# Sums of squares as 128 rows of 64 steps, two buffers for norms and masked scores, new orders in the mixer and the feed-forward stage

## The chip, the cores and the metric

The kernel runs on one core of a Trainium2 chip. The metric is the device time of one execution in microseconds (us). The engines are PE (TensorE: matmuls, with its weight loads shown apart as PEld), DVE (VectorE), ACT (ScalarE), POOL (GpSimd) and SP (SyncE, which here only issues transfers). Each takes its instructions in order and waits for others through semaphores; ACT, POOL and SP also issue DMAs.

## The reference

Eight rows of 512 steps by 256 channels pass a state-space mixer and a feed-forward layer, each behind a layernorm and followed by one. Cut to what matters:

```
x = x + layernorm(attn(layernorm(x)))          # x: 8 rows of 512 steps x 256
x = x + layernorm(ffn(layernorm(x)))

attn:  proj = x @ W_in.T                        # gate 512, value 512, 64 step parameters
       value = silu(dw_bias + sum(xp[:, k:k + T] * dw_weight[:, k] for k in range(4)))
       dt = clip(softplus(params[..., 0] + dt_bias), 1e-4, 0.1)
       bc = (value @ W_bc.T).reshape(B, T, 32, 4, 32)
       bc = bc / (sqrt(sum(bc * bc, axis=-1)) + 1e-8)
       per step:  z = S * (z - dt * A * s + dt * (Bz u));  s = s + dt * z + dt * (Bx u)
                  y = Cz . z + Cx . s
       out = ((y + skip * value) * silu(gate)) @ W_out.T
ffn:   out = gelu(x @ ternary(W1).T + b1) @ ternary(W2).T + b2
```

`Bz, Bx, Cz, Cx` are the four parts of `bc`, 32 heads by 32 states each, every one divided by its own norm over the 32 states.

## The kernel before

Three stages run one after the other. `project` makes the value, the gate and the step sizes, row after row, and leaves them in DRAM. The change does not touch it. `mix` is the mixer, `ffn` the output projection, the residual and the feed-forward layer.

In `mix` the 32 heads are 8 groups of 4; a group fills 128 partitions (4 heads by 32 states). A row is worked in two halves of four groups ("first" to "first + 3"), and a pass over a half is called a phase here: 16 phases in all. In a phase the DVE works on the half at hand and prepares the next one (its first group is called "then" in the code).

Products: PE multiplies `w_bc` by `valT` in units, four units (j = 0..3) per group, each four matmuls of 128x512 (L700). ACT takes each unit out of PSUM twice, squared into `sq` and as it is into `raw` (`evacuate`). PE runs 21 units ahead of the phase.

Norms: after the first unit of the next group PE sums the squares (`sum_squares`, L685: four matmuls with `head_sum`, 32 rows by 512 steps each, into 128 partitions of which 16 matter). ACT takes the square root (L825) into `rows`. SP packs the 16 rows of 512 into `compact`, 128 rows of 64, by four DMAs (`compact_norms`). DVE adds the epsilon, inverts, and multiplies by `factor` (`scales`, L1027 to L1034). SP stores `compact` to DRAM, waits for it, and loads it back spread over the partitions into `scale`: four DMAs for the B parts (`input_scales`), and, once DVE has used those, four for the C parts (`output_scales`). DVE multiplies `raw` by it: `scale_inputs` (L1042) and `scale_outputs` (L1050). There is one `compact`, one `scale` and one `factor`.

The rest of a phase: DVE runs 128 small steps of a recurrence (`step_psi`, L1016 and L1020) woven between its other work by a count of nominal costs (`advance`). `keys` makes the B side of a group (L1079, L1083); PE transposes it (L722) and forms the state terms (L738). `det_sums`, `coefficients` and `states` (L1156 to L1165) make the block states of the half, which ACT spreads into `Xb` (L877). `queries` makes the C side (L1093 to L1116). PE then computes the scores of a group (`scores_and_unit`, L759, with one product unit in two pieces between), DVE multiplies them by the causal mask (`mask`, L1124) into the one tile `g`, and PE makes the outputs (`outputs`: L778 from `g`, L784 from `Xb`). Scores of a group wait for the mask of the group before; the mask waits for the outputs of the group before, as there is one `g`.

What sets the order is the program order that is written out in `phase` for DVE and in the bodies of the other engines.

In `ffn` one row after the other is gated (`y * gate + svg`, two operations of 128x2048 on POOL, L1387 and L1389), projected (L1407), normalised and added (`first_residual`), normalised again (`second_norm`), split into a high and a low part, multiplied (L1436), passed through gelu on ACT (L1494), split again, multiplied by the second weight (L1449), given its bias, normalised and added (the end of the DVE body). A loop over pairs of rows runs this, with the first and last two rows written out.

## Time and profile before

| what | us |
|---|---|
| median of 3 runs | 2638.85 |
| lowest, highest | 2637.96, 2643.87 |
| the profiled execution | 2637.77 |
| its span in the trace | 2636.1 |
| of it `ffn` | 2308 to 2636 |
| det inverse (one per phase), first to last | 449.63 to 2239.5 |

The profiled execution lies 1.1 us under the median and 1.7 us over its own span. Busy times are for one engine; an engine that waits is idle in them. A number in square brackets behind a row of a timeline is the idle time before it, with what ended it.

### The profile page before, as it was taken

The numbers are of one execution on the slowest core, as the hardware profiler recorded it, in microseconds if no ns is written. First come the engines' busy times: TensorE is split into PE (matmuls) and PEld (weight loads), VectorE is DVE, ScalarE is ACT, GpSimd is POOL, SyncE is SP. The second block draws the span as 40 slices with busy tenths as digits, with TensorE's granted clock in tenths as the row PEclk, the third lists the DMA queues.
The fourth block names the chain that finished last, engine by engine and source line by source line (L and its number), as shares of the span: only waits on it lengthen the run. The fifth ranks groups of instructions, "written<-read, shape, count | busy, mean of one in ns | idle before, by whom it ended". The sixth has DMA issues, their size and how long they took to land. (4 is left out here: it accounts for less than half of the span.)

```text
span 2636.1 us, 66597 instructions
## 1 busy us (share of the span) xinstructions
PE 2092.6 (79%) x25890; PEld 1258.7 (48%) x25890; DVE 1921.2 (73%) x4396; ACT 956.8 (36%) x1905; POOL 385.6 (15%) x604
## 2 busy tenths in 40 slices
PE   5777485887888988888878789998988887728886
PEld 2333132454454545444544445454544446626675
DVE  5777257786869686878878697968778797456775
ACT  3555222333333333343433333343333332104444
POOL 0000111111111111111111111111111110042210
PEclk9888697988889889988888888898898985568887
DMA  3555542534353535444353535454453533073300
GB/s 96 172 171 163 148 127 82 134 100 131 96 137 99 131 103 136 109 111 131 104 129 97 135 95 130 115 135 111 107 134 101 137 83 85 14 253 127 127 25 24
DMA packets 240466, 306.05 MB, mean 116 GB/s; under 512 B 124960, under 2 KB 141344, under 8 KB 231968
## 3 DMA queue, kind: packets, MB, share of 16 engines
q1 hardware_dynamic: 134496, 152.84, 20.2%
q10 hardware_dynamic: 85056, 94.40, 12.8%
q0 software_dynamic: 20608, 54.56, 8.2%
q8 instruction: 212, 3.47, 0.6%
q14 instruction: 94, 0.77, 0.1%
HBM read 240.85 MB, written 57.68 MB: 113 GB/s over the span
## 5 line engine op out<-in xcount | busy, mean ns | idle before, releaser
L700 PE MATMUL m_ps_a<-m_valT,m_w_bc 128*128 128x512 f32 x2048 | 1037.3, 651 | 59.5 <-DMA m_valT<-scratch_valT 49.2
L700 PEld LDWEIGHTS m_ps_a<-m_valT,m_w_bc 128*128 128x128 f32 x2048 | 397.3, 206 | 472.9 <-issue 443.7
L651 POOL DMA_DIRECT2D m_shear<-scratch_shear x512 | 274.3, 537 | 1564.8 <-DVE m_psi L1020 1452.8
L835 ACT ACTIVATE m_sq<-m_ps_a 128x512 f32<-128x512 f32 x256 | 153.1, 598 | 651.7 <-PE m_ps_a L700 651.7
L759 PE MATMUL m_ps_g<-m_raw 32*64 32x64 f32 x8192 | 185.9, 249 | 166.9 <-DVE m_g L1124 141.3
L1020 DVE TENSOR_TENSOR m_psi<-m_psi,m_prod 128x128 f32<-128x128 f32 x1024 | 294.0, 287 | 19.6
L1016 DVE TENSOR_TENSOR m_prod<-m_psi,m_shear 128x128 f32<-128x128 f32 x1024 | 293.0, 286 | 18.0
L759 PEld LDWEIGHTS m_ps_g<-m_raw 32*64 32x64 f32 x8192 | 165.0, 159 | 268.4 <-issue 265.9
L1042 DVE TENSOR_TENSOR m_raw<-m_raw,m_scale 128x1024 f32<-128x1024 f32 x64 | 78.4, 1224 | 239.0 <-DMA m_scale<-scratch_norm 230.3
L784 PE MATMUL m_ps_k<-m_raw,m_Xb 128*112 128x64 f32 x1024 | 177.1, 306 | 0.0
L1079 DVE TENSOR_TENSOR m_part<-m_raw,m_psi 128x1024 f32<-128x1024 f32 x128 | 155.6, 1218 | 13.7 <-issue 13.2
L224 PE MATMUL ps_w<-p_xnT,w_in 128*128 128x512 f32 x256 | 130.5, 663 | 41.1 <-ACT vraw L282 36.0
L1110 DVE TENSOR_TENSOR m_part<-m_raw,m_psi 128x1024 f32<-128x1024 f32 x128 | 155.6, 1218 | 0.1
L784 PEld LDWEIGHTS m_ps_k<-m_raw,m_Xb 128*112 128x112 f32 x1024 | 150.9, 216 | 8.5 <-issue 3.7
L837 ACT ACTIVATE m_raw<-m_ps_a 128x512 f32<-128x512 f32 x256 | 152.5, 596 | 0.0
L897 ACT ACTIVATE m_y<-m_ps_y 112x256 f32<-112x256 f32 x64 | 24.6, 384 | 305.1 <-PE m_ps_k L784 305.1
L1124 DVE TENSOR_TENSOR m_g<-m_ps_g,m_causal 128x1024 f32<-128x1024 f32 x64 | 78.0, 1219 | 74.4 <-PE m_ps_k L784 74.3
L784 PE MATMUL m_ps_y<-m_raw,m_Xb 128*112 128x64 f32 x768 | 130.4, 303 | 0.0
L877 ACT ACTIVATE m_Xb<-m_X 32x224 f32<-32x224 f32 x256 | 98.7, 386 | 74.9 <-DVE m_X L1165 71.8
L1050 DVE TENSOR_TENSOR m_raw<-m_raw,m_scale 128x1024 f32<-128x1024 f32 x64 | 78.1, 1220 | 60.5 <-DMA m_scale<-scratch_norm 60.5
L784 PEld LDWEIGHTS m_ps_y<-m_raw,m_Xb 128*112 128x112 f32 x768 | 114.1, 218 | 0.0
L224 PEld LDWEIGHTS ps_w<-p_xnT,w_in 128*128 128x128 f32 x256 | 52.2, 212 | 115.8 <-issue 66.0
(147 smaller groups left out, 2847.5 us busy)
## 6 DMA issues: line engine op xcount, KB each, us to landing
m_scale<-scratch_norm SPq DMA_DIRECT2D x512, 128.0 KB
m_w_bc<-in_w_bcT ACTq DMA_DIRECT2D x252, 256.0 KB, 3.5
m_shear<-scratch_shear POOLq DMA_DIRECT2D x512, 64.0 KB, 2.9
m_det<-scratch_ab POOLq DMA_DIRECT2D x64, 256.0 KB, 5.6
scratch_yT<-m_y ACTq DMA_DIRECT2D x64, 224.0 KB, 2.8
...
```

What stands on the lines that cost most here:

```text
L224: mm = pe.matmul(ps_w[i % BANKS].ap(), w_in[:, k, col:col + P], xnT[:, k, :], start=(k == 0), stop=(k == KD - 1))
L651: pool.dma_start(shear[h * N:(h + 1) * N, w % 2].rearrange("p k g t -> p k (g t)"), spread(src)).then_inc(into.sem, into.step)
L700: mm = pe.matmul(ps_a[j % 2].ap(), w_bc[:, j, kt, :], valT[:, kt, :], start=(kt == 0), stop=(kt == KI - 1))
L759: mm = pe.matmul(ps_g[odd * C:(odd + 1) * C, at:at + C], raw[heads, group, p_, cols], raw[heads, group, NJ - 1 - p_, cols], start=(p_ == 0 ...
L784: mm = pe.matmul(ps_y[c % 2][0:ROWS, c // 2 * C:(c // 2 + 1) * C], Xb[:, c - 1, p_, :], raw[:, group, NJ - 1 - p_, c * C:(c + 1) * C], sta ...
L835: act.activation(sq[:, j, :], ps_a[j % 2].ap(), ACT.Square).then_inc(sq_ready.sem, sq_ready.step)
L837: act.activation(raw[:, group % HG, j, :], ps_a[j % 2].ap(), ACT.Copy).then_inc(raw_ready.sem, raw_ready.step)
L877: ins = act.activation(Xb[heads, :, :, h * N:h * N + DH], X[heads, 0:NC - 1, :, group % HALF, :], ACT.Copy)
L1016: dve.tensor_tensor(prod.ap().rearrange("p k g r -> p (k g) r"), psi_kt[of_half][:, :, t, :], window.unsqueeze(2).to_broadcast([P, 2 * HAL ...
L1020: ins = dve.tensor_tensor(psi_t[of_half][:, :, :, t + 1, :], psi_t[of_half][:, :, :, t, :], prod[:, ::-1, :, :], ALU.add)
L1079: dve.tensor_tensor(in_pairs(part[:, k]), pairs(raw[:, slot, k, :]), psi[:, half % 2, k, g_, :, at:at + C, :], ALU.mult).then_inc(own.sem, ...
L1110: dve.tensor_tensor(in_pairs(part[:, k]), pairs(raw[:, group, 3 - k, :]), psi[:, half, k, g_, :, 1:, :], ALU.mult).then_inc(own.sem, own.o ...
```

## The change

In `mix`:
- `sum_squares` uses eight matrices `of_segment`, each of which puts the four heads into other output rows, and 32 matmuls of 64 columns in place of 4 of 512. The result stands in PSUM as 128 rows of 64 steps, the layout of `compact`.
- The square root writes `compact` at once; `compact_norms` and `rows` are gone. `compact` has two buffers, and the square root waits for the store of two groups before.
- The masked scores alternate between `g` and the memory of `kT`, and the mask waits for the outputs of two groups before.
- DVE's order in a phase is new: scalings of the next half come earlier, and the first mask stands inside `states`, after its fourth block.
- SP loads `valT` of the next row tile by tile as the last unit lets each go, behind the scale loads of "then + 2".

In `ffn`: the loop is written out; gating is on DVE and POOL has nothing left; weights are loaded from ACT's queue; the ternary step takes two operations instead of three; the second product comes in two halves with bias and moments after each; the last normalisation of a row moves behind the start of the next.

The diff, cut:

```diff
@@ mix: tiles @@
+        of_segment = sb("of_segment", [P, N // HP, N])
...
-        rows_ = sb("rows", [P, T])
-        compact = sb("compact", [P, SEG])
+        compact = sb("compact", [P, 2, SEG])
...
+        masked = [g.ap(), kT.ap().rearrange("p a (b h c) -> p a b h c", b=2, h=HP)]
@@ mix: SP @@
-                def compact_norms(b, group):
-                    sp.wait_ge(norm_ready.sem, norm_ready.at(b, group))
-                    for j in range(NJ):
-                        sp.dma_start(compact[j * N:(j + 1) * N, :],
-                                     rows_[j * N:j * N + HP, :].rearrange("h (s t) -> h s t", t=SEG)
-                                     ).then_inc(compact_in.sem, compact_in.step)
...
                 def load_valT(b):
                     for kt in range(KI):
+                        if not (isinstance(b, int) and b == 0):
+                            sp.wait_ge(val_used.sem, val_used.at(b - 1, kt)) if kt < KI - 1 else sp.wait_ge(a_made.sem, a_made.at(b - 1, UNITS - 1))
                         sp.dma_start(valT[:, kt, :], dram["valT"][b, :, kt, :]).then_inc(val_in[kt].sem, val_in[kt].step)
...
-                    compact_norms(b, group)
...
                     sp.dma_start(dram["norm"][group % 2].rearrange("r (s t) -> (r s) t", t=SEG),
-                                 compact.ap()).then_inc(rows_stored.sem, rows_stored.step)
+                                 compact[:, group % 2, :]).then_inc(rows_stored.sem, rows_stored.step)
...
                             norm_rows(b, then + 2)
+                            input_scales(b, then + 2)
                         if half == 0 and not last:
-                            sp.wait_ge(a_made.sem, a_made.at(b, UNITS - 1))
                             load_valT(b + 1)
                         if more:
-                            input_scales(b, then + 2)
                             output_scales(b, then + 2)
                             norm_rows(b, then + 3)
-                        if more:
                             input_scales(b, then + 3)
                             output_scales(b, then + 3)
@@ mix: PE @@
-                    for j in range(NJ):
-                        mm = pe.matmul(ps_s[j * N:(j + 1) * N, :], head_sum.ap(), sq[:, j, :],
-                                       start=True, stop=True, skip_group_check=True)
+                    for s in range(N // HP):
+                        for j in range(NJ):
+                            mm = pe.matmul(ps_s[j * N:(j + 1) * N, 0:SEG], of_segment[:, s, :], sq[:, j, s * SEG:(s + 1) * SEG],
+                                           start=(s == 0), stop=(s == N // HP - 1), skip_group_check=True)
                     mm.then_inc(sums_made.sem, sums_made.step)
...
+                        if unit == UNITS - 1 and kt < KI - 1:
+                            mm.then_inc(val_used.sem, val_used.step)
...
-                                          u[rows, s, tile, h * DH:(h + 1) * DH], g[rows, h % 2, h // 2, tile, :],
+                                          u[rows, s, tile, h * DH:(h + 1) * DH], masked[s % 2][rows, h % 2, h // 2, tile, :],
@@ mix: ACT @@
+                for s in range(N // HP):
+                    act.activation(of_segment[:, s, s::N // HP], head_sum[:, 0:HP], ACT.Copy).then_inc(segments_ready, 1)
...
-                    act.wait_ge(compact_in.sem, compact_in.at(b, group * NJ - 1))
-                    act.activation(rows_.ap(), ps_s.ap(), ACT.Sqrt).then_inc(norm_ready.sem, norm_ready.step)
+                    act.wait_ge(rows_stored.sem, rows_stored.at(b, group - 2))
+                    act.activation(compact[:, group % 2, :], ps_s[:, 0:SEG], ACT.Sqrt).then_inc(norm_ready.sem, norm_ready.step)
@@ mix: DVE @@
+                dve.memset(of_segment.ap(), 0.0).then_inc(const_set, 1)
...
-                    dve.wait_ge(compact_in.sem, compact_in.at(b, (group + 1) * NJ - 1))
-                    dve.tensor_scalar(compact.ap(), compact.ap(), NORM_EPS, None, ALU.add).then_inc(own.sem, own.one())
+                    dve.wait_ge(norm_ready.sem, norm_ready.at(b, group))
+                    v = compact[:, group % 2, :]
+                    dve.tensor_scalar(v, v, NORM_EPS, None, ALU.add).then_inc(own.sem, own.one())
                     advance(140)
...
-                    dve.wait_ge(y_made.sem, y_made.at(b, group - 1))
-                    dve.tensor_tensor(g.ap().rearrange("p a h c t -> p (a h c) t"),
+                    dve.wait_ge(y_made.sem, y_made.at(b, group - 2))
+                    dve.tensor_tensor(masked[group % 2].rearrange("p a h c t -> p (a h c) t"),
...
+                        if c == NC // 2 - 1:
+                            between()
...
                     det_sums(b, half, advance)
                     if more:
                         scale_outputs(b, then, advance)
+                        scales(b, then + 1, advance)
                     keys(b, first + 3, advance)
                     queries(b, first, advance)
+                    if more:
+                        scale_inputs(b, then + 1, advance)
                     queries(b, first + 1, advance)
                     if more:
-                        scales(b, then + 1, advance)
+                        scale_outputs(b, then + 1, advance)
+                        scales(b, then + 2, advance)
                     coefficients(b, half, advance)
-                    states(b, half, advance)
-                    mask(b, first, advance)
+                    states(b, half, advance, lambda: mask(b, first, advance))
                     if more:
-                        scale_inputs(b, then + 1, advance)
+                        scale_inputs(b, then + 2, advance)
                     queries(b, first + 2, advance)
                     mask(b, first + 1, advance)
                     if more:
-                        scale_outputs(b, then + 1, advance)
-                        scales(b, then + 2, advance)
+                        scale_outputs(b, then + 2, advance)
+                        scales(b, then + 3, advance)
                     queries(b, first + 3, advance)
-                    if more:
-                        scale_inputs(b, then + 2, advance)
                     mask(b, first + 2, advance)
                     if more:
-                        scale_outputs(b, then + 2, advance)
-                        scales(b, then + 3, advance)
+                        scale_inputs(b, then + 3, advance)
                     advance(OF_PHASE)
-                    if more:
-                        scale_inputs(b, then + 3, advance)
                     mask(b, first + 3, advance)
                     if more:
+                        scale_outputs(b, then + 3, advance)
                         keys(b, then, stepping(b, half + 2, not last))
-                        scale_outputs(b, then + 3, advance)
@@ ffn: PE @@
+                def hidden(b, f):
...
+                def second(b, half_):
+                    for t in range(2 * half_, 2 * half_ + 2):
                         for f in range(KF):
                             for part in (gh, gl):
-                                mm = pe.matmul(ps_2[t // 2][:, t % 2, :], part[:, f, t * P:(t + 1) * P], t2[:, f, :],
+                                mm = pe.matmul(ps_2[half_][:, t % 2, :], part[:, f, t * P:(t + 1) * P], t2[:, f, :],
                                                start=(f == 0 and part is gh), stop=(f == KF - 1 and part is gl),
                                                skip_group_check=True)
                     mm.then_inc(o2_made.sem, o2_made.step)
-                rows(pe, body)
+                def body(b, s, left):
+                    pe.wait_ge(xl_ready.sem, xl_ready.at(b, KD - 1))
+                    for f in range(2):
+                        hidden(b, f)
+                    if left > 1:
+                        for t in range(2):
+                            project_out(b + 2, s, t)
+                    for f in range(2, KF):
+                        hidden(b, f)
+                    if left > 1:
+                        for t in range(2, TT):
+                            project_out(b + 2, s, t)
+                    pe.wait_ge(gl_ready.sem, gl_ready.at(b, KF - 1))
+                    pe.wait_ge(o2_ready.sem, o2_ready.at(b, -1))
+                    second(b, 0)
+                    if left:
+                        transpose_xn(b + 1)
+                    second(b, 1)
+                rows(body)
@@ ffn: ACT @@
+                for n, (dst, name) in enumerate(((w1, "w1T"), (w2, "w2T"))):
+                    act.dma_start(dst.ap(), a[name].rearrange("(k p) o -> p k o", p=P)).then_inc(weight_in[n], 16)
@@ ffn: DVE @@
+                def gating(b):
+                    s = b % 2
+                    dve.wait_ge(y_in[s].sem, y_in[s].at(b // 2, y_in[s].per - 1))
+                    dve.tensor_tensor(y[s].ap(), y[s].ap(), gate[s].ap(), ALU.mult).then_inc(own.sem, own.one())
+                    dve.wait_ge(own.sem, own.n)
+                    dve.tensor_tensor(y[s].ap(), y[s].ap(), svg[s].ap(), ALU.add).then_inc(gated.sem, gated.step)
...
+                def second_bias(b, half_):
+                    dve.wait_ge(o2_made.sem, o2_made.at(b, half_))
...
+                def second_residual(b):
...
+                    dve.tensor_tensor(res.ap(), x1[b % 2].ap(), on.ap(), ALU.add).then_inc(res_ready.sem, res_ready.step)
+                    dve.wait_ge(res_ready.sem, res_ready.at(b, 0))
...
-                    dve.tensor_scalar(above.ap(), w, half[:, n:n + 1], None, ALU.is_gt).then_inc(own.sem, own.one())
                     dve.tensor_scalar(below.ap(), w, nhalf[:, n:n + 1], None, ALU.is_lt).then_inc(own.sem, own.one())
                     dve.wait_ge(own.sem, own.n)
-                    dve.tensor_tensor(tern.ap().rearrange("p k o -> p (k o)"), above.ap(), below.ap(),
-                                      ALU.subtract).then_inc(ternary_ready, 1)
+                    dve.scalar_tensor_tensor(out=tern.ap().rearrange("p k o -> p (k o)"), in0=w, scalar=half[:, n:n + 1],
+                                             in1=below.ap(), op0=ALU.is_gt, op1=ALU.subtract).then_inc(ternary_ready, 1)
                     dve.wait_ge(ternary_ready, n + 1)
+                    if n == 0:
+                        gating(1)
...
+                def body(b, s, left):
+                    if b:
+                        second_residual(b - 1)
                     for f in range(KF):
                         dve.wait_ge(gh_ready.sem, gh_ready.at(b, f))
                         dve.tensor_tensor(gl[:, f, :], g[:, f, :], gh[:, f, :].bitcast(F32), ALU.subtract).then_inc(gl_ready.sem, gl_ready.step)
                         if left and f == KF // 2 - 1:
-                            first_residual(b + 1, 1 - s, i + s)
+                            first_residual(b + 1, 1 - s)
                     if left:
                         second_norm(b + 1, 1 - s)
                     if left > 1:
                         projection_moments(b + 2)
+                    second_bias(b, 0)
                     if left:
                         low_part(b + 1)
...
+                    if left > 2:
+                        gating(b + 3)
+                    second_bias(b, 1)
```

How this moves instructions. DVE, in the middle of a phase, behind the queries of the second group. `m_compact` are the norms, `m_end` and `m_coef` the coefficients. Before:

```order
L1016 TENSOR_TENSOR m_prod<-m_psi,m_shear 128x128
L1020 TENSOR_TENSOR m_psi<-m_psi,m_prod 128x64x2
L1026 ISA
L1027 TENSOR_SCALAR m_compact<-m_compact 128x64
L1030 RECIPROCAL m_compact<-m_compact 128x64
L1016 TENSOR_TENSOR m_prod<-m_psi,m_shear 128x128
L1032 ISA
L1034 TENSOR_TENSOR m_compact<-m_compact,m_factor 128x64
L1133 ISA
L1135 TENSOR_TENSOR m_end<-m_det,m_e_end 128x28
```

Now, at the same place:

```order
L1051 TENSOR_TENSOR m_raw<-m_raw,m_scale 128x1024
L1016 TENSOR_TENSOR m_prod<-m_psi,m_shear 128x128
L1020 TENSOR_TENSOR m_psi<-m_psi,m_prod 128x64x2
L1026 REGISTER_ALU
L1028 TENSOR_SCALAR m_compact<-m_compact 128x64
L1031 RECIPROCAL m_compact<-m_compact 128x64
L1016 TENSOR_TENSOR m_prod<-m_psi,m_shear 128x128
L1033 ISA
L1035 TENSOR_TENSOR m_compact<-m_compact,m_factor 128x64
L1020 TENSOR_TENSOR m_psi<-m_psi,m_prod 128x64x2
L1134 ISA
L1136 TENSOR_TENSOR m_end<-m_det,m_e_end 128x28
```

Before, these norms are those of "then + 1". Now both scalings of "then + 1" are done by here, and the norms are those of "then + 2".

DVE, in `ffn`, from the end of one row's second product to the low parts of the next row. Before:

```order
L1563 TENSOR_TENSOR f_xl<-f_ps_x,f_xh 128x512 x2
L1609 TENSOR_TENSOR f_o<-f_ps,f_b 128x512 x2
L1523 BN_STATS f_stats<-f_o 128x6 x4
L1526 BN_AGGR f_mv<-f_stats 128x2 x4
L1616 RECIPROCAL f_rstd<-f_sd 128x4
L1531 TENSOR_SCALAR f_o<-f_o,f_mv,f_rstd 128x256 x4
L1621 TENSOR_TENSOR f_res<-f_x,f_o 128x1024
L1623 ISA
L1598 TENSOR_TENSOR f_gl<-f_g,f_gh 128x512 x4
```

Now:

```order
L1566 TENSOR_TENSOR f_o<-f_ps,f_b 128x512
L1575 BN_STATS f_stats<-f_o 128x6 x2
L1578 BN_AGGR f_mv<-f_stats 128x2 x2
L1561 TENSOR_TENSOR f_xl<-f_ps_x,f_xh 128x512 x2
L1533 TENSOR_TENSOR f_y<-f_y,f_gate 128x2048
L1535 TENSOR_TENSOR f_y<-f_y,f_svg 128x2048
L1566 TENSOR_TENSOR f_o<-f_ps,f_b 128x512
L1575 BN_STATS f_stats<-f_o 128x6 x2
L1578 BN_AGGR f_mv<-f_stats 128x2 x2
L1641 ISA
L1583 RECIPROCAL f_rstd<-f_sd 128x4
L1522 TENSOR_SCALAR f_on<-f_o,f_mv,f_rstd 128x256 x4
```

The bias and moments are in two halves, and the gating of a later row stands between them.

## Rows read from the trace of the kernel before

**Rows 1.** The page: busy time, share of the span, instructions.
```profile
PE 2092.6 (79%) x25890; PEld 1258.7 (48%) x25890; DVE 1921.2 (73%) x4396; ACT 956.8 (36%) x1905; POOL 385.6 (15%) x604
```
**Rows 2.** Timeline, ACT: start, us, operation. First and last full half row.
```profile
449.63 1.91 ACT L855 ACTIVATE m_det<-m_det 128x2048 f32<-128x2048 f32 x1 [4.68 <-DVE m_det L1057]
...
2135.81 1.91 ACT L855 ACTIVATE m_det<-m_det 128x2048 f32<-128x2048 f32 x1
```
**Rows 3.** Groups by line and shape: busy, mean ns | idle before, releasers.
```profile
L759 PE MATMUL m_ps_g<-m_raw 32*64 32x64 f32 x8192 | 185.9, 249 | 166.9 <-DVE m_g L1124 141.3 <-issue 24.3 <-DVE m_raw L1116 0.3
...
L1042 DVE TENSOR_TENSOR m_raw<-m_raw,m_scale 128x1024 f32<-128x1024 f32 x64 | 78.4, 1224 | 239.0 <-DMA m_scale<-scratch_norm 230.3 <-ACT m_raw L837 6.9 <-issue 1.8
L1050 DVE TENSOR_TENSOR m_raw<-m_raw,m_scale 128x1024 f32<-128x1024 f32 x64 | 78.1, 1220 | 60.5 <-DMA m_scale<-scratch_norm 60.5
L1124 DVE TENSOR_TENSOR m_g<-m_ps_g,m_causal 128x1024 f32<-128x1024 f32 x64 | 78.0, 1219 | 74.4 <-PE m_ps_k L784 74.3
...
L778 PE MATMUL m_ps_y<-m_g,m_u 64*16 64x64 f32 x2048 | 47.8, 241 | 68.8 <-DVE m_g L1124 68.8
```
**Rows 4.** Windows, one half row: PE, PEld, DVE, ACT, POOL busy, clock, DMA.
```profile
1418.70:1542.20 123.50, 102.14 (x1521) 59.10 (x1520) 94.83 (x222) 43.71 (x94) 19.28 (x37) 0.90 0.45 119
```
**Rows 5.** Timeline, DVE, 1400 to 1495: norms and scalings; idle before, releaser.
```profile
1400.47 0.23 DVE L1034 TENSOR_TENSOR m_compact<-m_compact,m_factor 128x64 f32<-128x64 f32 x1
...
1409.88 1.23 DVE L1042 TENSOR_TENSOR m_raw<-m_raw,m_scale 128x1024 f32<-128x1024 f32 x1 [3.83 <-DMA m_scale<-scratch_norm]
...
1472.13 0.23 DVE L1034 TENSOR_TENSOR m_compact<-m_compact,m_factor 128x64 f32<-128x64 f32 x1
...
1486.37 1.23 DVE L1042 TENSOR_TENSOR m_raw<-m_raw,m_scale 128x1024 f32<-128x1024 f32 x1 [6.22 <-DMA m_scale<-scratch_norm]
...
1493.67 1.23 DVE L1050 TENSOR_TENSOR m_raw<-m_raw,m_scale 128x1024 f32<-128x1024 f32 x1 [3.56 <-DMA m_scale<-scratch_norm]
```
**Rows 6.** Timeline, PE, 1387 to 1455: the clock after a wait.
```profile
1387.59 0.95 PE L784 MATMUL m_ps_k<-m_raw,m_Xb 128*112 128x64 f32 x4
...
1392.16 5.60 PE L700 MATMUL m_ps_a<-m_valT,m_w_bc 128*128 128x512 f32 x8 [0.64 <-issue]
...
1398.47 3.60 PE L700 MATMUL m_ps_a<-m_valT,m_w_bc 128*128 128x512 f32 x8
...
1454.79 1.98 PE L759 MATMUL m_ps_g<-m_raw 32*64 32x64 f32 x64 [7.70 <-DVE m_g L1124]
```
**Rows 7.** PE: sums of squares; a window with L778 alone; L784 at full clock.
```profile
1431.72 1.06 PE L685 MATMUL m_ps_s<-m_sq,m_head_sum 128*32 128x512 f32 x8
...
1341.20:1342.10 0.90, 0.90 (x66) 0.80 (x65) 0.90 (x3) 0.80 (x2) 0.00 (x0) 1.00 0.07 15
...
1465.36 0.56 PE L784 MATMUL m_ps_k<-m_raw,m_Xb 128*112 128x64 f32 x4
1465.75 0.56 PE L784 MATMUL m_ps_y<-m_raw,m_Xb 128*112 128x64 f32 x4
```
**Rows 8.** Timeline, start and end of `mix`: ACT, then DVE.
```profile
324.88 0.60 ACT L825 ACTIVATE m_rows<-m_ps_s 128x512 f32<-128x512 f32 x1
...
330.11 0.20 DVE L1027 TENSOR_SCALAR m_compact<-m_compact 128x64 f32<-128x64 f32 x1 [22.37 <-DMA m_compact<-m_rows]
...
2271.83 1.23 DVE L1124 TENSOR_TENSOR m_g<-m_ps_g,m_causal 128x1024 f32<-128x1024 f32 x1 [6.28 <-PE m_ps_k L784]
```
**Rows 9.** `ffn`: seven rows' window; timelines of DVE and POOL.
```profile
2374.00:2599.70 225.70, 182.60 (x921) 154.36 (x922) 158.99 (x347) 107.16 (x171) 45.90 (x10) 0.88 0.24 83
...
2341.80 2.29 DVE L1582 TENSOR_TENSOR f_t<-f_above,f_below 128x2048 fp32r<-128x2048 f32 x1
...
2474.70 7.92 DVE L1531 TENSOR_SCALAR f_o<-f_o,f_mv,f_rstd 128x256 f32<-128x256 f32 x4
...
2542.87 1.38 DVE L1531 TENSOR_SCALAR f_o<-f_o,f_mv,f_rstd 128x256 f32<-128x256 f32 x4
...
2472.66 4.51 POOL L1387 TENSOR_TENSOR f_y<-f_y,f_gate 128x2048 f32<-128x2048 f32 x1 [23.74 <-DMA f_y<-scratch_yT]
```

163 lines of the change are left out of this document (70 added, 93 removed).

## The prediction

> **What bounds the kernel now.** I read the page's busy times first [rows 1]: PE 79% and DVE 73% of the span, ACT 36%. No engine is full, so the time is made of waits between the first two. Next the timeline of ACT, for the length of a phase: the determinant's inverse runs once in each, at 449.63 and at 2135.81, with 14 intervals between [rows 2]. That is 1686.2/14 = 120.4 us a phase. In one window of a phase (123.5 us, a little over the mean) PE is busy 102.14 and DVE 94.83, with the granted clock at 0.90 on the mean, between its levels of 0.5 and 1 (1.2 and 2.4 GHz) [rows 4].
>
> Then the groups by line, for what ends the idle time [rows 3]. There are 16 half rows, so each sum is divided by 16. DVE waits for `scale` before L1042 and L1050: (230.3 + 60.5)/16 = 18.2 us. It waits before the mask L1124 for PE's outputs: 74.3/16 = 4.6. PE waits for masks before L759 and L778: (141.3 + 68.8)/16 = 13.1. The reader should see a circle: PE waits for a mask, and the mask stands on DVE behind scalings that wait for a transfer.
>
> The timeline of DVE shows why [rows 5]. Norms are done (L1034) at 1400.47 and the scaling starts at 1409.88: 9.2 us for storing and loading back. The next pair takes 14.0 (1472.36 to 1486.37). After the B parts, the C parts wait for a second load: from the end of L1042 at 1487.60 to 1493.67, 6.1 us. The norms stand directly ahead of their own scaling, with too little between to cover 9 to 14 us. Over a set I take 17.5 for a steady phase, not 18.2, as the set in the prologue has less work beside it; and 3.5 for the masks, not 4.6, since one mask of the last half row alone waited 6.28 [rows 8].
>
> Without them DVE needs 120.4 - 17.5 - 3.5 = **99.4 us** a phase. PE without its mask waits needs 120.4 - 13.1 = 107.3. Part of this is the low clock that is granted behind a wait [rows 6]: four L784 take 0.95 against 0.56 [rows 7], and eight L700 took 5.60 and the next eight 3.60 us. Some seven such groups of L784 and one of L700 make 7 x 0.39 + 2.0 = 4.7. So PE's floor is 107.3 - 4.7 = **102.6**. Both floors lie close together, 18 to 21 under 120.4.
>
> **The change, part by part.** *Order of scalings on DVE.* Norms now stand a group of work ahead of the scaling that they serve: the norms of "then + 1" before `keys` and a `queries`, and its scalings behind them; the C scaling comes a `queries` after the B one. Those are the pieces that cover a load. What is left, by laying the measured chains (9.2 to 14.0, and 6.1) beside the work that now stands between: "then + 1" is covered. "then + 2" has only `coefficients`, `states` and one mask between, about 11 us against 14: 3.0 left. "then + 3" has `queries` and a mask: 3.0. Its C part has the steps that are left and a mask of 1.22 against 6.1, of which I leave 1.5. Sum 7.5 in place of 17.5.
>
> *Mask inside `states`, and two buffers.* The mask waits for the outputs of two groups before, so the 3.5 go. It stands one scaling later and half of `states` earlier than before, about the same time on DVE; so PE's first wait of a phase (7.70 before L759 in [rows 6]) stays at 4 to 8, and those for later masks shrink. These are on PE; DVE at 99.4 + 7.5 = 106.9 is above PE's 102.6, so they lie beside it. **Phase: 107 us.** The gain is 14 x (120.4 - 107) = **188**.
>
> *Sums of squares.* Before: four matmuls of 512 columns, eight records, 1.06 us together [rows 7], which shows that the four output groups run side by side. Now 32 matmuls of 64 columns, 64 records, each with another weight. No row has this form. The cheapest neighbour is L778, small matmuls that each bring their own weight: a window with it alone has 66 records in 0.90 us, 14 ns each [rows 7]; 64 of them give 0.9. The dear end is L784, 64 columns on all 128 rows: groups of four start 0.39 us apart (1465.36, 1465.75) [rows 7], 98 ns a record; 64 of them make 6.3 us a group, 21 a phase more than now. I take 1.1, as the nearest row is L778: the new matmuls go to several output groups in turn as its do. So **no change**; the dear end is a rival below. By the Trainium skill ("TensorE: Matmul & The Clock Gate", Part 3, Packing small matmuls, under What overlaps and what doesn't) a weight load overlaps with matmuls in flight only where its row group is another one; all 64 loads here span all 128 rows, so by it they would queue, near the dear end, 2618, and the phase would not get shorter. The window of L778, whose loads within a half share their rows, speaks against it.
>
> The square root writes 64 columns instead of 512: 0.60 before [rows 8], about 0.3 now, on ACT at 36%, nothing. SP loses four DMAs a group and DVE the wait for them. In the prologue this is on the path: sqrt ends at 325.48 and the norms are used at 330.11 [rows 8], 4.6 us. **5**. The `valT` loads, tile by tile, save about 2 us before every other phase's products on PE, beside DVE: nothing; a load placed behind scale loads on SP is not waited for in 100 us.
>
> *Last half rows.* The interval behind 2135.81 has the same four chains and masks: two thirds of a steady phase's gain, **9**. In the last there are no scalings, only masks like the 6.28 [rows 8], and the half clock behind each: **8**.
>
> *`ffn`.* Seven rows take 225.70 us, 32.2 each, with DVE busy 158.99 and PE 182.60 at a clock of 0.88 [rows 9]. So neither is full and the row is a chain: gelu, low parts, second product, bias, moments, normalise, and the next row. While POOL gates, DVE's normalise takes 7.92 for four operations; without it 1.38 [rows 9]: 6.5 a row, on the chain. The two gating operations come to DVE. No row shows them there; the same shape, L1582, takes 2.29 [rows 9], so 4.6 a row, placed between the two halves of the second product, where DVE waits for PE. DVE's idle time is (225.7 - 159.0)/7 = 9.5 a row, which holds 4.6; if that cover were gone, they cost all of it. Bounds for a row: 32.2 - 6.5 = 25.7 with all hidden; 25.7 + 4.6 = 30.3 with none. In the middle stands 28.0: by halves, the product 2 can run beside bias and moments of half 1, which hides most, yet PE's 26.1 busy and its waits behind a restart leave some. 7 x 4.2 = **30**. Head and tail lose one ternary operation of 2.29 twice, slowed normalises, and part of a last chain: 0 to 20, I take **10**.
>
> The sum: 188 + 5 + 9 + 8 + 30 + 10 = 250. From the profiled 2637.8 this gives **2388**. The median shown lies 1.1 above that execution, which I leave out.
>
> **The rivals.** *A, PE decides.* All scale waits vanish and DVE has 99.4; PE needs 102.6. For it: both floors are near each other, and later masks no longer wait. Against it: a chain of 14 us has not got 14 us of work in two of three places. Time: 14 x 17.8 = 249, with 62 for the rest, 311: **2327**; with 10 more in `ffn` 2317.
>
> *B, the loads in a row.* There is still one `scale`. SP stores, waits, loads, waits until DVE has used it, loads again; four groups in series, each 14.0 + 1.2 + 6.1 + 1.2 and about 1 for the handover, 23.5, hence 94 of a phase. A store waits for DVE's norms, which the new order puts right behind the C scaling of the group before, so nothing of a chain runs beside the next. For it: 94 is close to 107, and chains of 9.2 and 14.0 stand side by side [rows 5], so they may be long. Phase 112: 14 x 8.4 = 118 + 62 = 180: **2458**; with `ffn` at 25 only, 2473.
>
> *C, dear sums, slower than before.* Each of the 64 loads stands before its matmul as in L784. At 98 ns PE has 102.6 + 4 x 5.2 = 123.4: 42 lost, 62 gained outside the phases, 2618, hardly a gain. With the clock at its low level a record would take 98 x 0.95/0.56 = 166 ns [rows 6, 7], 10.6 us a group, and the phase 102.6 + 38 = 140.6: 14 x 20.2 = 283 lost, 62 gained, **2859**. The kernel as a whole is slower from a phase of 124.8, which is 6.6 us a group. For it: every load has all 128 rows, unlike L778. Against: four output groups side by side.
>
> *D, the mixer keeps its waits.* DVE, being earlier at the norms, now waits for them instead of `scale` (PE has not summed them yet): a phase of 118, 14 x 2.4 = 34 + 62: **2542**. Against it: products run 21 units ahead.
>
> **How the numbers follow.** Forecast 0.56 (its own spread 2350 to 2425, from phases of 104.5 to 109 and `ffn` of 25 to 45 us), A 0.15, B 0.20, C 0.04, D 0.05. The range takes in the forecast, A and B with their far ends: 2317 to 2473, and leaves C and D out, with the tails 0.2 at most. A measurement can tell about 0.2% from no change, 5 us here. Faster 0.95, within it 0.01 (C near its turning point), slower 0.04 (C).
>
> **What the profile after would show.** The interval between two inverses: 107, from 102.6 (A) to 112 (B); 118 is D. The four sums of squares' group: 1.1 us; 6 or more is C. Scalings' waits: none at "then + 1", 3 at "then + 2" and "then + 3", 1.5 at the last C part, 7.5 in all against 17.5. The mask's wait for PE's outputs gone, PE's for a mask left before L759 once a phase. In `ffn` no POOL, the normalise at 1.4, a gating operation at 2.3, a row at 28. I am wrong if the waits for `scale` stay near 17, if PE is the later of the two throughout, or if sums cost microseconds.

## The result and the profile after

| what | before | after |
|---|---|---|
| median, us | 2638.55 (4 runs) | 2404.47 (4 runs, 2401.71 to 2417.8) |
| ratio, 95% interval | 1 | 0.912, 0.908 to 0.916 |
| profiled execution, us | 2637.77 | 2401.71 |
| phase, mean of 14 | 120.4 | 107.8 |
| 15th interval of the inverse | 103.7 | 93.6 |
| last inverse to the first instruction of `ffn` | 69.6 | 62.8 |
| `ffn`, to the end of its last result on DVE | 323.5 | 287.0 |

The forecast was 2388, the time is 2404: a gain of 234 us where 250 were forecast. I begin with the timeline of ACT, the inverse of the determinant: the first, the fifteenth and the sixteenth. It answers to [rows 2].

```profile
444.26 1.91 ACT L854 ACTIVATE m_det<-m_det 128x2048 f32<-128x2048 f32 x1 [6.05 <-DVE m_det L1058]
...
1953.42 1.91 ACT L854 ACTIVATE m_det<-m_det 128x2048 f32<-128x2048 f32 x1 [2.62 <-DVE m_det L1058]
...
2047.03 1.91 ACT L854 ACTIVATE m_det<-m_det 128x2048 f32<-128x2048 f32 x1
```

(1953.42 - 444.26)/14 = 107.8. The first inverse comes at 444.26 for 449.63, which is the prologue's 5.4 us. Next the groups by line and shape, which answer to [rows 3]; behind the bar stand busy time, mean ns of one, and idle time before with what ended it.

```profile
L756 PE MATMUL m_ps_g<-m_raw 32*64 32x64 f32 x8192 | 177.8, 243 | 105.6 <-DVE m_g L1125 83.1 <-issue 20.2 <-DVE m_raw L1117 1.0
...
L1043 DVE TENSOR_TENSOR m_raw<-m_raw,m_scale 128x1024 f32<-128x1024 f32 x64 | 78.2, 1223 | 114.5 <-DMA m_scale<-scratch_norm 112.4 <-ACT m_raw L836 2.1
L1051 DVE TENSOR_TENSOR m_raw<-m_raw,m_scale 128x1024 f32<-128x1024 f32 x64 | 78.1, 1221 | 49.6 <-DMA m_scale<-scratch_norm 44.9 <-ACT m_raw L836 4.8
L680 PE MATMUL m_ps_s<-m_sq,m_of_segment 128*32 128x64 f32 x4096 | 70.4, 220 | 0.7 <-ACT m_sq L834 0.7
L1125 DVE TENSOR_TENSOR m_g<-m_ps_g,m_causal 128x1024 f32<-128x1024 f32 x32 | 39.0, 1219 | 1.0 <-PE m_ps_g L756 1.0
L1125 DVE TENSOR_TENSOR m_kT<-m_ps_g,m_causal 128x1024 f32<-128x1024 f32 x32 | 39.0, 1218 | 12.3 <-PE m_ps_g L756 12.3
```

The waits for `scale` fell from 290.8 us to 157.3, some 38 of which stand in the prologue, as before. The mask no longer waits for the outputs of a group (74.3 before); 13.3 are left, for scores. PE waits 83.1 us for masks in place of 210.1, and 80.4 of them are for the first mask of a phase. The window of one phase (after: 106.88 us, to lay beside [rows 4]) has PE busy 97.66 and DVE 92.11, at a granted clock of 0.95 for 0.90; the second row, for `ffn`, has seven rows' worth of work and POOL empty.

```profile
core 0: us, PE busy (x) PEld busy (x) DVE busy (x) ACT busy (x) POOL busy (x), PEclk, DMA share, GB/s
1199.41:1306.29 106.88, 97.66 (x1745) 58.63 (x1744) 92.11 (x217) 42.26 (x94) 17.72 (x34) 0.95 0.46 125
2181.50:2376.00 194.50, 169.30 (x922) 134.95 (x920) 161.69 (x374) 107.47 (x175) 0.00 (x0) 0.99 0.27 95
```

Where the waits that are left stand shows in DVE's timeline (compare [rows 5]). The first three rows are the fourth group of a half, the last three the first group of the next half.

```profile
1251.55 0.23 DVE L1035 TENSOR_TENSOR m_compact<-m_compact,m_factor 128x64 f32<-128x64 f32 x1
...
1265.57 1.23 DVE L1043 TENSOR_TENSOR m_raw<-m_raw,m_scale 128x1024 f32<-128x1024 f32 x1 [4.23 <-DMA m_scale<-scratch_norm]
...
1271.51 1.23 DVE L1051 TENSOR_TENSOR m_raw<-m_raw,m_scale 128x1024 f32<-128x1024 f32 x1 [1.08 <-DMA m_scale<-scratch_norm]
...
1288.17 0.19 DVE L1028 TENSOR_SCALAR m_compact<-m_compact 128x64 f32<-128x64 f32 x1
...
1289.15 0.23 DVE L1035 TENSOR_TENSOR m_compact<-m_compact,m_factor 128x64 f32<-128x64 f32 x1
...
1297.44 1.23 DVE L1043 TENSOR_TENSOR m_raw<-m_raw,m_scale 128x1024 f32<-128x1024 f32 x1 [2.70 <-DMA m_scale<-scratch_norm]
```

Over the 14 phases the mean wait at each place is: B part of the first group 3.0, of the second and third 0, of the fourth 3.4; C parts 0, 0, 0.6 and 1.5. That is 8.5 us a phase. DVE waits for PE only 0.5 us a phase (0.3 for norms, 0.2 for scores), while PE waits 4.8 for masks: DVE sets the pace.

In `ffn` the result of one row is made 27.8 us after that of the row before, and the gating stands on DVE at 2.3 us an operation:

```profile
2200.98 2.28 DVE L1533 TENSOR_TENSOR f_y<-f_y,f_gate 128x2048 f32<-128x2048 f32 x1
2203.30 2.29 DVE L1535 TENSOR_TENSOR f_y<-f_y,f_svg 128x2048 f32<-128x2048 f32 x1
...
2209.25 1.23 DVE L1588 TENSOR_TENSOR f_res<-f_x,f_on 128x1024 f32<-128x1024 f32 x1
2237.04 1.23 DVE L1588 TENSOR_TENSOR f_res<-f_x,f_on 128x1024 f32<-128x1024 f32 x1
```

The head, up to the first result, took 107.5 us before and 99.4 after; the seven rows between the first and the last result took 214.8 and 186.4 us.

### The profile page after: what moved, and what is told of

The parts are those of the page before. It is cut to its first block and busy times, and to the rows that moved or that the text cites. A ratio compares the mean times of both kernels' runs of the same rounds, so it can differ in the third digit from the quotient of the medians.

```text
span 2400.0 us, 73278 instructions
## 1 busy us (share of the span) xinstructions
PE 2009.4 (84%) x29474; PEld 1234.3 (51%) x29474; DVE 1911.9 (80%) x4411; ACT 932.8 (39%) x1913; POOL 311.4 (13%) x588
## 3 DMA queue, kind: packets, MB, share of 16 engines
q10 hardware_dynamic: 86368, 96.50, 14.1%
## 5 line engine op out<-in xcount | busy, mean ns | idle before, releaser
L695 PE MATMUL m_ps_a<-m_valT,m_w_bc 128*128 128x512 f32 x2048 | 1011.8, 636 | 56.6 <-DMA m_valT<-scratch_valT 39.3
L695 PEld LDWEIGHTS m_ps_a<-m_valT,m_w_bc 128*128 128x128 f32 x2048 | 385.9, 200 | 455.5 <-issue 438.0
L756 PE MATMUL m_ps_g<-m_raw 32*64 32x64 f32 x8192 | 177.8, 243 | 105.6 <-DVE m_g L1125 83.1
L756 PEld LDWEIGHTS m_ps_g<-m_raw 32*64 32x64 f32 x8192 | 157.4, 154 | 188.4 <-issue 183.9
L1043 DVE TENSOR_TENSOR m_raw<-m_raw,m_scale 128x1024 f32<-128x1024 f32 x64 | 78.2, 1223 | 114.5 <-DMA m_scale<-scratch_norm 112.4
L781 PE MATMUL m_ps_k<-m_raw,m_Xb 128*112 128x64 f32 x1024 | 156.4, 279 | 0.1
L781 PEld LDWEIGHTS m_ps_k<-m_raw,m_Xb 128*112 128x112 f32 x1024 | 131.1, 191 | 7.4 <-issue 0.8
L781 PE MATMUL m_ps_y<-m_raw,m_Xb 128*112 128x64 f32 x768 | 114.9, 276 | 0.0
L1384 PE MATMUL f_ps_o<-f_w_out,f_y 128*128 128x256 f32 x256 | 64.0, 407 | 47.8 <-DVE f_y L1535 47.8
L719 PE MATMUL m_ps_k<-m_ident,m_raw 128*128 128x128 f32 x512 | 71.1, 285 | 34.2 <-DVE m_raw L1084 32.0
L781 PEld LDWEIGHTS m_ps_y<-m_raw,m_Xb 128*112 128x112 f32 x768 | 98.7, 191 | 0.0
## 6 DMA issues: line engine op xcount, KB each, us to landing
m_scale<-scratch_norm SPq DMA_DIRECT2D x512, 128.0 KB
```

What stands on the lines that cost most here:

```text
L695: mm = pe.matmul(ps_a[j % 2].ap(), w_bc[:, j, kt, :], valT[:, kt, :], start=(kt == 0), stop=(kt == KI - 1))
L756: mm = pe.matmul(ps_g[odd * C:(odd + 1) * C, at:at + C], raw[heads, group, p_, cols], raw[heads, group, NJ - 1 - p_, cols], start=(p_ == 0 ...
L781: mm = pe.matmul(ps_y[c % 2][0:ROWS, c // 2 * C:(c // 2 + 1) * C], Xb[:, c - 1, p_, :], raw[:, group, NJ - 1 - p_, c * C:(c + 1) * C], sta ...
```

## The experiments

My theory: a phase takes the larger of two times, DVE's work with the waits for `scale` that the order leaves (99.4 + 8.5 us), and PE's floor (the phase that PE needs when it waits for no mask) of 102.6; the gain is in the order. Rivals: the new form of the sums of squares carries it; PE decides already; the small matmuls are dear. Ratios are to the kernel before.

### One stage alone

The first run has `ffn` as before, the second has everything but `ffn` as before.

> The kernel after with ffn as before. The traces put mix and what lies ahead of it at 199 us of the gain (2309.2 against 2109.8 for the first instruction of ffn) and ffn at 37. If the two stages are independent, this is 2404 + 37 = 2441 us, a ratio of 0.925 to the kernel before. If the new ffn owes part of its gain to what mix leaves (or the other way round), the sum of this run's gain and that of the run with ffn alone differs from 234 us by more than 5.

> The kernel before with ffn as after: 2638.5 - 36.5 = 2602 us, ratio 0.986, the row at 27.8 us as in the kernel after. Rival: the head of ffn depends on what the mixer leaves in the queues, then below 2590 or above 2612.

Measured: 2433.5 us (ratio 0.923, 0.917 to 0.929) and 2605.5 us (0.989, 0.983 to 0.995). Against the 2638.9 beside them the gains are 205 and 33, in sum 239 where both together gave 234. I had expected 2441 and 2602. The stages are independent within the scatter of these runs; it is wide here, the four times of the first run lie between 2424.9 and 2454.1. The row of `ffn` is 27.8 us in the second run too.

### DVE's old order, twice

In the kernel after, DVE's phase is written in the old order:

```diff
                     det_sums(b, half, advance)
                     if more:
                         scale_outputs(b, then, advance)
-                        scales(b, then + 1, advance)
                     keys(b, first + 3, advance)
                     queries(b, first, advance)
-                    if more:
-                        scale_inputs(b, then + 1, advance)
                     queries(b, first + 1, advance)
                     if more:
-                        scale_outputs(b, then + 1, advance)
-                        scales(b, then + 2, advance)
+                        scales(b, then + 1, advance)
...
```

> The kernel after with DVE's old order in a phase (norms directly ahead of their scalings, first mask behind the states), everything else kept: new sums of squares, two buffers for norms and for masks. If the order carries the gain, the waits for scale come back to about 17 us a phase, less the mask's wait of 3.5: phase 107.8 + 9 = 117, 14 x 9 = 126 us more, 2530. Rival, the sums' new layout and the freed queue of SP carry it: the waits for scale stay near 8 us, at most 2440.

Measured: 2571.8 us (0.979, 0.971 to 0.986), 167 more than after and 40 more than I expected, the phase at 119.4. The groups name a wait that I had made myself; the first row is the kernel after, the second this run:

```profile
L695 PE MATMUL m_ps_a<-m_valT,m_w_bc 128*128 128x512 f32 x2048 | 1011.8, 636 | 56.6 <-DMA m_valT<-scratch_valT 39.3 <-issue 17.2
```

```profile
L695 PE MATMUL m_ps_a<-m_valT,m_w_bc 128*128 128x512 f32 x2048 | 1030.9, 646 | 163.3 <-DMA m_valT<-scratch_valT 152.4 <-issue 10.8
```

SP loads `valT` behind the store of "then + 2", and the old order makes that store late. So the run was repeated with SP's loads at their old place too:

> As the run with DVE's old order, with SP's valT loads also at their old place, ahead of the store of then + 2. In that run PE waited 152 us for valT (39 in the kernel after, nearly all of it at the start), 16 us in every other phase, as the loads stood on SP behind a store whose norms the old order makes late. If that wait is on the path: 2572 - 40 = 2530, the phase at 117, as first expected. If it lies beside DVE's waits for scale, the phase stays at 119 and the time at 2572, and the order alone costs 11.6 us a phase.

Measured: 2538.6 us (0.962, 0.959 to 0.965), the phase at 116.9 (inverses at 448.65 and 2085.25). The wait for `valT` is gone, and the waits for `scale` are those of before:

```profile
L695 PE MATMUL m_ps_a<-m_valT,m_w_bc 128*128 128x512 f32 x2048 | 1030.3, 646 | 47.9 <-DMA m_valT<-scratch_valT 38.1 <-issue 9.7
...
L1043 DVE TENSOR_TENSOR m_raw<-m_raw,m_scale 128x1024 f32<-128x1024 f32 x64 | 78.3, 1223 | 231.4 <-DMA m_scale<-scratch_norm 231.4
L1051 DVE TENSOR_TENSOR m_raw<-m_raw,m_scale 128x1024 f32<-128x1024 f32 x64 | 78.2, 1221 | 79.5 <-DMA m_scale<-scratch_norm 77.7 <-issue 1.8
```

DVE's order, with SP's loads in the order that suits it, is worth 134 us. The place of one load on SP's queue, in the wrong order, is worth 33.

### The old sums of squares

Four matmuls of 512 columns, one `compact` and its four DMAs, in DVE's new order:

```diff
-                    for s in range(N // HP):
-                        for j in range(NJ):
-                            mm = pe.matmul(ps_s[j * N:(j + 1) * N, 0:SEG], of_segment[:, s, :], sq[:, j, s * SEG:(s + 1) * SEG],
+                    for j in range(NJ):
+                        mm = pe.matmul(ps_s[j * N:(j + 1) * N, :], head_sum.ap(), sq[:, j, :],
...
-                    dve.wait_ge(norm_ready.sem, norm_ready.at(b, group))
+                    dve.wait_ge(compact_in.sem, compact_in.at(b, (group + 1) * NJ - 1))
```

> The kernel after with the sums of squares as before (4 matmuls of 512 columns), one compact tile and its four DMAs per group; DVE's new order kept. The norms stand right behind the output scaling of the group before, and the packing DMAs are issued behind its loads: I expect 1 to 2 us of wait per group for compact, 4 to 8 a phase, 56 to 112 us more, 2460 to 2515. Rival, the layout saves nothing in steady state (the DMAs are hidden beside the loads): only the prologue's 5 us, 2410. Rival on the other side: the 64 small matmuls cost PE time that four large ones do not, then this is below 2400.

Measured: 2479.2 us (0.940, 0.934 to 0.946), 75 more, the phase at 113.1. DVE waits for the packing:

```profile
L1033 DVE TENSOR_SCALAR m_compact<-m_compact 128x64 f32<-128x64 f32 x64 | 12.1, 189 | 87.2 <-DMA m_compact<-m_rows 87.2
```

22.0 of it stand in the prologue; a phase has 4.7, inside the 4 to 8 expected, and 1.0 more for `scale`. In the old order (the run with `ffn` alone) the same line waits 36.0 us in all, again 22.0 of it in the prologue, and 0.9 a phase. And the kernel with DVE's old order but the new sums and two masks has a phase of 116.9, 3.6 under that run's 120.5, which is about what its masks wait for PE (3.5). So the packing costs next to nothing in the old order, as my sum had it, and 75 us in the new one. The new order still gains without it (2479.2 against 2638.9), but gives up a good part.

### The floor without the waits for `scale`

This kernel leaves out the loads of `scale`, in which ones stand instead, and so the division by the norms in its result.

```diff
-                    load_scales(group % 2, 1)
+                    sp.sem_inc(scale_in.sem, HP * scale_in.step)
```

> The kernel after without any load of scale: the tile holds ones, SP signals DVE as soon as the store is issued (B part) or the B part is scaled (C part). Leaves out the division by the norms in the result and 512 DMAs. It measures the floor without the waits for scale (8.2 us a phase in the trace of after). By the prediction DVE then needs 99.4 to 99.6 a phase and PE 102.6: phase 102.6 to 103, 14 x 5 = 70 and some 30 in the prologue less, 2300 to 2340. If a phase stays at 106 or more, PE's floor was put too low and the remaining waits for scale are worth nothing.

Measured: 2278.5 us (0.862, 0.858 to 0.866), 126 less than after. The inverses are at 406.34 and 1837.03, so the phase is 102.2, where my count of PE's floor said 102.6. The profiled executions differ by 119: 38 in the prologue, 78 in the 14 phases and 5 in the 15th interval, with 3 given back behind it. It lies below the 2300 to 2340 expected, as the first two are 8 us each more than I had put and the third was not in my sum. The 102.2 are not PE's floor pure, though. PE still waits 53.2 us for masks, 3.1 a phase, and DVE 3.5 a phase for PE (1.5 for norms, 2.0 for scores): it is what the two need together in this order.

```profile
L755 PE MATMUL m_ps_g<-m_raw 32*64 32x64 f32 x8192 | 166.9, 234 | 66.2 <-DVE m_g L1125 53.2 <-issue 11.7 <-DVE m_kT L1125 0.9
```

### The price of the small matmuls, and PE's slack

Two runs make the sums dearer. The first exchanges the two loops, so that all eight matmuls into one output group (32 of the 128 rows of PSUM) follow each other; the second makes the sums three times over.

```diff
-                    for s in range(N // HP):
-                        for j in range(NJ):
+                    for j in range(NJ):
+                        for s in range(N // HP):
```

> The kernel after with the loops of the 64 small matmuls exchanged: all eight of one output group in a row, then the next output group, in place of the four output groups in turn. Same work, same result. If the low price (17 ns a record) rests on the turn of output groups, each record costs what L784 costs, 98 ns: 6.3 us a group, PE 102.6 + 21 = 123, 2404 + 15 x 15.6 = 2638. If a matmul of 64 columns is priced by its columns alone and the order is free: 1.1 us a group, 2404. A load of 32 columns for 112 would give something between: 98 x 32/112 = 28 ns, 1.8 us a group, at most 2 us a phase more, 2404 to 2435.

> The kernel after with the sums of squares made three times over (192 small matmuls for 64; the sum is then three times as large). PE gets 2.2 us more per group, 8.8 a phase. If DVE bounds the phase at 107.8 and PE's floor is 102.6, the new floor is 111.4 and the phase grows by 3.6: 2404 + 15 x 3.6 = 2458. If PE bounds it already, the whole 8.8 show: 2404 + 132 = 2536. If neither, since PE's waits for masks absorb it: under 2420.

Measured: 2435.0 us (0.923, 0.918 to 0.927) and 2499.3 us (0.947, 0.942 to 0.952). PE's timeline of one group, first of after, then with the loops exchanged:

```profile
1276.76 1.10 PE L680 MATMUL m_ps_s<-m_sq,m_of_segment 128*32 128x64 f32 x64
```

```profile
1269.87 3.18 PE L680 MATMUL m_ps_s<-m_sq,m_of_segment 128*32 128x64 f32 x64
```

17 ns a record in turn, 50 ns in a row: the turn of output groups saves a factor of 2.9. The dear end of my bounds, 98 ns, is not reached even so. I had expected 1.1, 1.8 or 6.3 us a group; it is 3.18. The time is at the upper end of what I had put to 1.8.

For the phase this is 4 x 2.08 = 8.3 us more on PE. It grew from 107.8 to 110.3, and the floor of 102.2 with 8.3 on it is 110.5. That fits some 5.6 us of room for PE in the kernel after, where it waits 4.8 a phase for masks.

The run with three sums missed all three of its expectations (2458, 2536, under 2420) and first seems to speak against that: PE busy with L680 rose by 120.4 us, 7.5 a phase, which gives a floor of 109.7, but the phase is 114.5. Its groups show idle time with no releaser, which the trace calls "issue". The last row is the kernel after:

```profile
L680 PE MATMUL m_ps_s<-m_sq,m_of_segment 128*32 128x64 f32 x12288 | 190.8, 220 | 30.0 <-issue 29.3 <-ACT m_sq L834 0.7
...
L735 PE MATMUL m_ps_k<-m_u,m_kT 64*32 64x16 f32 x7168 | 82.5, 185 | 63.5 <-issue 58.6 <-ACT m_kT L860 4.9
```

```profile
L735 PE MATMUL m_ps_k<-m_u,m_kT 64*32 64x16 f32 x7168 | 77.1, 184 | 23.9 <-ACT m_kT L860 13.7 <-issue 10.2
```

After has no "issue" at L680. The added 77.7 are 4.9 a phase: 102.2 + 7.5 + 4.9 = 114.6. So the run added more than I meant to; both runs then agree with one floor. In this run PE waits only 6.5 us in all for masks: here it is PE that sets the pace.

### One tile of masked scores

```diff
-        masked = [g.ap(), kT.ap().rearrange("p a (b h c) -> p a b h c", b=2, h=HP)]
+        masked = [g.ap(), g.ap()]
...
-                    dve.wait_ge(y_made.sem, y_made.at(b, group - 2))
+                    dve.wait_ge(y_made.sem, y_made.at(b, group - 1))
```

> The kernel after with one tile for the masked scores, so that a mask waits for the outputs of the group before. The trace of before had 3.3 us a phase of this wait. If DVE bounds the phase and the wait comes back in full, 15 x 3.3 = 50 more, 2454. If the new distance between masks (scalings earlier, masks later) hides it, under 2415. A circle (mask waits for outputs, outputs wait for the mask) would cost more than its wait: above 2470.

Measured: 2455.4 us (0.929, 0.925 to 0.933), 51 more, the phase at 111.5.

```profile
L1125 DVE TENSOR_TENSOR m_g<-m_ps_g,m_causal 128x1024 f32<-128x1024 f32 x64 | 78.1, 1221 | 107.3 <-PE m_ps_k L781 107.3
```

The wait is 107.3 us, more than the 74.3 of before [rows 3], and it stands elsewhere: 5.3 us a phase before the last mask, where before had 2.8 before the second. The waits for `scale` fell by 13 us beside it. The time is what was expected.

The prices of the order (134), the packing (75) and the second tile (51) sum to more than the 205 that `mix` gained. Each is taken with the other parts in place, so they don't add up.

### Gating back on POOL

> The kernel after with the gating in ffn back on POOL, the rest of the new ffn kept. By the prediction DVE gets 4.6 us a row back and loses up to 6.5 where an operation of it meets POOL's (normalise 7.92 for 1.38), if that meeting is on the path: 2405 + 7 x 2 = 2419, up to 2445 with the second shared operation. If the gain of the new ffn comes from the halves of the second product and the order, POOL's gating is free: 2405 or less, as DVE has 4.6 us less to do.

Measured: 2440.0 us (0.926, 0.923 to 0.929), 36 more, in the upper part of what was expected; the profiled executions differ by 29. DVE's timeline in `ffn`: a normalise while POOL gates, then the stored results of rows with gating beside them (first two intervals) and without (the last two).

```profile
2247.49 8.85 DVE L1534 TENSOR_SCALAR f_on<-f_o,f_mv,f_rstd 128x256 f32<-128x256 f32 x4
...
2256.38 1.23 DVE L1600 TENSOR_TENSOR f_res<-f_x,f_on 128x1024 f32<-128x1024 f32 x1
2289.25 1.23 DVE L1600 TENSOR_TENSOR f_res<-f_x,f_on 128x1024 f32<-128x1024 f32 x1
2321.98 1.23 DVE L1600 TENSOR_TENSOR f_res<-f_x,f_on 128x1024 f32<-128x1024 f32 x1
2347.50 1.22 DVE L1600 TENSOR_TENSOR f_res<-f_x,f_on 128x1024 f32<-128x1024 f32 x1
2372.92 1.23 DVE L1600 TENSOR_TENSOR f_res<-f_x,f_on 128x1024 f32<-128x1024 f32 x1
```

A row takes 32.8 us with POOL beside it and 25.5 without; on DVE the gating gives 27.8. From the first stored result to the last it is 200.7 us here, 214.8 before and 186.4 after: of the 28.4 us that the rows gain, 14.1 are the new loop's and 14.3 come from taking the gating off POOL. Ahead of the first result the latter is worth 12 us more, where the whole head gained 8: the rest of the new loop costs 4 there.

### Two attempts to remove the waits that are left

The first puts the norms of the second to fourth group one place earlier, behind the B scaling of the group before, with SP's order to match:

```diff
                     if more:
                         scale_inputs(b, then, advance)
+                        scales(b, then + 1, advance)
                     det_sums(b, half, advance)
                     if more:
                         scale_outputs(b, then, advance)
-                        scales(b, then + 1, advance)
...
```

> The kernel after with the norms of the next group put one place earlier on DVE (behind the B scaling of the group before instead of its C scaling) and SP's order to match, so that the store runs beside the C loads. If the chain of store and load behind the norms is what is left of the wait, 8.2 us a phase fall to 2 to 5, phase 103 to 105.5, 2365 to 2390. Rival: the norms are not ready there (PE has not summed them) or the single scale tile sets the pace: 2400 or more.

Measured: 2700.6 us (1.022, 1.018 to 1.027), 296 more than after and slower than before, the phase at 128.0. I had expected 2365 to 2390, with a rival of 2400 or more.

```profile
L1028 DVE TENSOR_SCALAR m_compact<-m_compact 128x64 f32<-128x64 f32 x64 | 12.4, 193 | 319.8 <-ACT m_compact L824 319.7
```

The waits for `scale` did fall (71.0 + 20.8 us), but DVE now waits 319.7 us for norms that PE has not summed. It is rival D of the prediction, a circle: DVE stands still ahead of the masks that PE waits for (254 us in place of 84), so PE is late with the next sums. The trace of after shows how near it was: the square roots of three groups (the third and fourth of one half, the first of the next), and DVE's use of the first two.

```profile
1216.77 0.22 ACT L824 ACTIVATE m_compact<-m_ps_s 128x64 f32<-128x64 f32 x1
...
1250.41 0.22 ACT L824 ACTIVATE m_compact<-m_ps_s 128x64 f32<-128x64 f32 x1 [2.37 <-PE m_ps_s L680]
...
1279.29 0.23 ACT L824 ACTIVATE m_compact<-m_ps_s 128x64 f32<-128x64 f32 x1
```

```profile
1224.73 0.19 DVE L1028 TENSOR_SCALAR m_compact<-m_compact 128x64 f32<-128x64 f32 x1
1250.66 0.20 DVE L1028 TENSOR_SCALAR m_compact<-m_compact 128x64 f32<-128x64 f32 x1
```

The norms of the fourth group are used 0.03 us after they are ready here, as in five of the 15 sets; the median is 1.0. Those of the next half's first group are ready 8.7 us ahead (used at 1288.17 above; median 8.0). Those of the third have such room too, but its B scaling waits for nothing. So I moved the norms of the first group, and for the fourth the scaling, not the norms:

```diff
                     if more:
+                        scales(b, then, advance)
+                    keys(b, first + 1, advance)
-                        scales(b, then, advance)
                     keys(b, first + 2, advance)
...
-                        scale_inputs(b, then + 3, advance)
                     advance(OF_PHASE)
                     mask(b, first + 3, advance)
                     if more:
-                        scale_outputs(b, then + 3, advance)
+                        scale_inputs(b, then + 3, advance)
                         keys(b, then, stepping(b, half + 2, not last))
+                        scale_outputs(b, then + 3, advance)
```

> The kernel after with the three waits for scale that are left moved under work: the norms of the first group of the next half go to the front of the phase, the B scaling of its fourth group behind the last mask, the C scaling behind the keys that follow. The waits there are 3.0, 3.4 and 1.3 us a phase. If they go and nothing takes their place, the phase falls from 107.8 to the floor that the run without loads showed, 102.2: 2404 - 15 x 4 to 5.5 = 2322 to 2345. If the norms are not ready at the front of the phase (in the trace of after they are there 9 us ahead of their use, the move takes 9) part is given back: 2345 to 2385. Slower than 2404 if the move makes DVE wait for norms as in the run with all norms earlier.

Measured: 2367.4 us (0.896, 0.891 to 0.900), 37 less than after and the fastest that computes everything; it is the upper part of what was expected, the phase at 105.5 (445.36 to 1922.21).

```profile
L1051 DVE TENSOR_TENSOR m_raw<-m_raw,m_scale 128x1024 f32<-128x1024 f32 x64 | 78.0, 1219 | 26.3 <-DMA m_scale<-scratch_norm 26.1
L1043 DVE TENSOR_TENSOR m_raw<-m_raw,m_scale 128x1024 f32<-128x1024 f32 x64 | 78.0, 1218 | 21.6 <-DMA m_scale<-scratch_norm 21.6
...
L1125 DVE TENSOR_TENSOR m_kT<-m_ps_g,m_causal 128x1024 f32<-128x1024 f32 x32 | 39.1, 1221 | 62.9 <-PE m_ps_g L756 62.9
...
L1028 DVE TENSOR_SCALAR m_compact<-m_compact 128x64 f32<-128x64 f32 x64 | 12.2, 190 | 68.5 <-ACT m_compact L824 68.1 <-DVE m_prod L1016 0.3
```

The waits for `scale` are down from 157 to 48 us, most of them in the prologue. DVE waits for PE instead: 48 us more for norms, 51 more for scores. The moved norms used up their room, they are now waited for 2.9 us a phase. PE still waits 4.0 a phase for the first mask, so neither engine decides alone, and the phase stays 3.3 over the 102.2 of the run without loads. The two moves were not tried apart.

## The prediction, point by point

It was right, and high in its gain by 16 us by the medians, by 14 on the profiled executions. I go by the terms of the sum, measured on the latter.

| term | forecast | measured |
|---|---|---|
| 14 phases | 188 | 177 |
| prologue | 5 | 5.4 |
| 15th interval | 9 | 10.1 |
| last half row | 8 | 6.8 |
| `ffn` | 40 | 36.5 |
| sum | 250 | 236 |

**Phases.** DVE without the waits for `scale`: 99.4 forecast, 107.8 - 8.5 = 99.3 by the same subtraction in the trace of after. The term that was mis-sized is the waits that are left, 8.5 for 7.5, which with rounding makes the 11 us. Their sum was near, their places were partly wrong. I put 3.0 at "then + 2", where there is none. I left out the wait of the next half's first group, 3.0, whose norms have one `keys` between them and the scaling, in the old order and the new; [rows 5] had it, with 3.83. Two errors cancelled here. The fourth group was right (3.4 and 1.5 for 3.0 and 1.5). Part of the even result is luck.

**Masks.** As forecast: the wait of DVE for outputs went, and PE waits for the first mask of a phase alone, 5.0 us, forecast 4 to 8. The run with one tile prices the second tile at 51 us.

**Sums of squares.** 1.1 us a group, forecast 1.1; rival C is out. The nearest row was the right one, and the reason given with it (several output groups in turn) was borne out by exchanging the loops. The Trainium skill ("TensorE: Matmul & The Clock Gate", Part 3) says that a weight load overlaps with matmuls in flight only where its row group is another one. This trace does not agree for this form: all weights span all rows, and 64 records take 1.10 us in turn and 3.18 in a row, so the measurement decides. The dear end that I had put beside this rule, 6.3 us, was reached in neither order.

**Nothing for the packing DMAs outside the prologue.** The term was right for the sum, and for the wrong reason: I took the DMAs as hidden and so without worth. They are hidden in the old order only. Kept in the new one they cost 75 us. The prediction priced each part against the kernel before, one by one, and had no term for what one part makes possible for the other.

**PE's floor.** 102.6 from the rows of before; the run without loads has a phase of 102.2, with 3.1 us of waits for masks still in it. So PE alone needs less there, and that the two numbers meet so closely is partly luck. Rival A, at 2327, did not come true because the waits did not vanish; the last run, at 2367, shows that about half of it was to be had. Rival B priced the chain of loads at 112 a phase. That much did not show: two of four B parts wait for nothing. How it came from 94 us of chains to a phase of 112 the prediction did not say. Rival D did not happen, but the run with earlier norms shows its mechanism, and the fourth group is often at its edge.

**`ffn`.** The row was forecast at 28.0 and takes 27.8 (194.5/7 in the window above, for 32.2 before). The lower bound, 25.7 with the gating hidden, is near what rows without any gating take, 25.5 with POOL's loop and 25.1 in after; the upper, 30.3, was reached by no row with the gating on DVE. In after, a row without gating takes 25.1 us (results at 2320.39 and 2345.49), so by that row 2.7 of the gating's 4.6 us show and 1.9 are hidden. What the halves of the second product do for that was not tried alone and stays open. The rows were forecast at 30 and gained 28, head and tail at 10 and gained 8. The first three intervals, beside which POOL had gated, gained 5.4 each; the fourth, which had no gating before and has it now, 0.3; the last three, which have none in either, 4.0 on the mean.
